# A decoder layer on one core: self attention's order within a period, and where cross attention's first pair begins

## The reference

```
x = x + self_attn(layernorm(x))               # scores / 4 + bias, causal, softmax, values, Wo
q, k, v = layernorm(x) @ Wq + bq, ctx @ Wk + bk, ctx @ Wv + bv
out = softmax(q k^T / 8) v @ Wo + bo + layernorm(x)
x = x + layernorm(out) * gamma + beta
x = x + fp8(layernorm(x)) @ fp8(kernel) + bias
```

## Time and profile before

| | |
|---|---|
| time, median of 3 runs | 1931.88 us (1915.99 to 1938.19) |
| the profiled execution, its time | 1929.99 us |
| its span | 1928.2 us |
| PE busy | 1758.9 us (91%) |
| DVE, ACT, POOL busy | 1289.3, 921.8 and 974.3 us |
| mean granted TensorE clock | 0.947 of full speed |

### The profile page before, as it was taken

How to read it: one execution, slowest core, us unless ns; L and a number is a source line. 1 busy time by engine, 2 the same in 40 slices (tenths; PEclk the granted TensorE clock), 3 DMA queues, 4 the chain that set the end, 5 groups by cost and what they waited for, 6 DMA issues and landing times.

```text
span 1928.2 us, 29741 instructions
## 1 busy us (share of the span) xinstructions
PE 1758.9 (91%) x10650; PEld 886.1 (46%) x10650; DVE 1289.3 (67%) x2503; ACT 921.8 (48%) x1866; POOL 974.3 (51%) x824
## 2 busy tenths in 40 slices
PE   7989988988998999999999999999999999999962
PEld 3544444434444544445545545545544554554421
DVE  5677777766733557756756655665665665678998
ACT  2346667656765243244444444445445445445531
POOL 1000000000001466558888888898898898882244
PEclk9879999889988899899999999999999999999985
DMA  4232311250011000000000000000000000000001
GB/s 115 35 36 36 35 18 19 36 98 2 1 47 42 11 0 1 1 11 4 1 10 4 1 10 4 1 11 1 4 10 1 4 1 1 4 11 23 1 28 38
DMA packets 29129, 34.48 MB, mean 18 GB/s; under 512 B 4290, under 2 KB 27139, under 8 KB 27523
## 3 DMA queue, kind: packets, MB, share of 16 engines
q1 hardware_dynamic: 28984, 32.59, 9.1%
HBM read 14.99 MB, written 4.19 MB: 10 GB/s over the span
## 4 chain that ended last, share of the span: by engine, by line
PE 76%; DVE 16%; issue 3%; ACT 3%; SPq 1%; POOL 1%; DMA 0%; POOLq 0%; ACTq 0%; DVEq 0%
PE psum L964 17%; PE psum L944 14%; PE psum L929 9%; DVE maxima L1229 8%; PE psum L850 7%; PE psum L762 6%; PE psum L800 4%; PE psum L825 4%; PE psum L987 3%; PE psum L917 3%; PE psum L862 2%; PE psum L975 2%; DVE parts_room L1323 1%; DVE stack_room L1279 1%; PE psum L877 1%
## 5 line engine op out<-in xcount | busy, mean ns | idle before, releaser
L1229 DVE TENSOR_REDUCE maxima<-psum 128x1 f32<-128x400 f32 (+5 forms) x1664 | 858.8, 578 | 315.2 <-PE psum L929 214.3
L737 POOL TENSOR_TENSOR parts_room<-parts_room,weights_room 128x512 f32<-128x512 f32 (+1 forms) x565 | 705.6, 1279 | 141.3 <-ACT weights_room L1119 141.3
L1119 ACT ACTIVATE weights_room<-psum 128x512 f32<-128x512 f32 (+1 forms) x757 | 405.8, 599 | 500.2 <-PE psum L944 423.4
L1047 ACT ACTIVATE weights_room<-psum 128x512 f32<-128x512 f32 (+3 forms) x640 | 300.1, 534 | 178.1 <-PE psum L825 99.5
L1436 POOL TENSOR_SCALAR rstd<-meanvar 128x2 f32<-128x2 f32 (+1 forms) x24 | 8.2, 343 | 650.7 <-DVE meanvar L1179 650.7
L944 PE MATMUL psum<-stack_room,dk_hi 64*128 64x512 f32 (+1 forms) x1408 | 264.5, 410 | 4.9 <-ACT weights_room L1119 4.8
L929 PE MATMUL psum<-k_later,stack_room 64*128 64x400 f32 (+1 forms) x896 | 243.6, 412 | 22.5 <-DVE stack_room L1279 14.6
L929 PEld LDWEIGHTS psum<-k_later,stack_room 64*128 64x128 f32 x896 | 129.0, 185 | 221.2 <-issue 121.9
L964 PE MATMUL psum<-weights_room,parts_room 128*64 128x512 f32 (+1 forms) x754 | 204.6, 610 | 0.0
L964 PE MATMUL psum<-weights_room,late_room 128*64 128x512 f32 (+1 forms) x760 | 203.9, 609 | 0.0
L825 PE MATMUL psum<-stack_room,stack_room 51*128 51x512 f32 (+3 forms) x640 | 140.1, 437 | 36.6 <-DVE maxima L1229 34.4
(11 more groups left out here) (133 smaller groups left out, 1907.7 us busy)
## 6 DMA issues: line engine op xcount, KB each, us to landing
stack_room<-parts_room SPq DMA_DIRECT2D x84, 128.0 KB
x_block<-x_dram SPq DMA_DIRECT2D x8, 512.0 KB, 4.7
x_middle<-x_block SPq DMA_DIRECT2D x4, 512.0 KB, 3.2
x_block<-x_middle SPq DMA_DIRECT2D x4, 512.0 KB, 3.8
out_dram<-x_block SPq DMA_DIRECT2D x8, 256.0 KB, 2.1
stack_room<-parts_room SPq DMA_DIRECT2D x24, 64.0 KB
parts_room<-ctx_dram SPq DMA_DIRECT2D x1, 1536.0 KB
stack_room<-shift_rows SPq DMA_DIRECT2D x64, 2.0 KB
```

Source lines behind the costliest of these rows:

```text
L737: engine.tensor_tensor(sum_[:kw, :], old[:kw, :], weights[u % NP_WEIGHTS][:kw, :], ALU.add) \
L1047: engine.activation(w_self[s % NW][:, m, 0:n], bank_of(use + m)[:, 0:n], ACT.Exp, scale=SELF_SCALE).then_inc(emptied(use + m), 1)
L1119: engine.activation(weights[u % NP_WEIGHTS][:kw, :], pair_scores[u % NSCORES][:kw, :], ACT.Exp, scale=CROSS_SCALE).then_inc(pair_exp, 1)
L1229: engine.tensor_reduce(maxima[:, p % 2, i // TB, n, i % TB, ch:ch + 1], bank_of(use + n)[:, 0:real - k0], AX.X, ALU.max) \
```

## The change

In pairs 1 to 6 of self attention both chunks of a period now stand between the two scores and the values, where one stood ahead of each of the scores. Beside self's last pair now lie: cross attention's keys of pair 0 (from the fifth step on), and in the second half the turning of block 0's normalised rows into a buffer of their own (`early_turn`, `first_rows`, since `norm_t` still holds self's output), block 0's queries of pair 0, and the 16 chunks of block 0. The clearing of the keys' last columns is a stage of its own (`key_pads`). The keys' rests, the clearing of the shifts, the row of shifts of block 0 and the turning of blocks 1 and 2 stay between the two attentions. The queries of blocks 1 to 3, the turning of block 3 and the bias of `resid` move beside block 0 of cross, and pair 1's keys and queries from beside block 0 to beside block 1. The waits of the copies follow the buffers that they write.

```diff
@@ -178,7 +178,15 @@
     def self_out(self, b):
         for half in range(2):
             self.put("self_project", b, half, banks=1)
-        self.after(2, lambda: self.put("self_norm", b))
+        self.after(2, lambda: self.self_norm(b))
+
+    def self_norm(self, b):
+        self.put("self_norm", b)
+        self.normed = b
+
+    def early_turn(self, c):
+        assert self.normed >= 0
+        self.put("early_turn", c, banks=1)
 
     def sweep2(self, p):
...
 
-    def pair_keys(self, p):
+    def pair_keys(self, p, rests=True):
         steps = []
         for b in range(NK):
             steps.append((1, lambda b=b: self.put("project_keys", p, b, banks=1)))
+            if not rests:
+                steps.append((0, lambda b=b: self.put("key_steps", p, b)))
+                continue
             for kind, late in (("key_steps", 1), ("key_rests", 2)):
                 if b >= late:
                     steps.append((0, lambda kind=kind, b=b - late: self.put(kind, p, b)))
-        return steps + [(0, lambda kind=kind, b=b: self.put(kind, p, b))
-                        for kind, b in (("key_steps", NK - 1), ("key_rests", NK - 2), ("key_rests", NK - 1))]
+        ends = (("key_steps", NK - 1), ("key_rests", NK - 2), ("key_rests", NK - 1)) if rests else ()
+        return steps + [(0, lambda kind=kind, b=b: self.put(kind, p, b)) for kind, b in ends]
+
...
@@ -370,27 +386,34 @@
                                for b in range(-(-S // BQ)) for c in range(DC)]
 
                 main = self.sweep2(p)
-                self.spread(main, self.mingled(self.sweep1(p + 1), context), [n for n in range(len(main)) if n % 3 < 2])
+                self.spread(main, self.mingled(self.sweep1(p + 1), context), range(2, len(main), 3))
             else:
-                self.interleave(self.sweep2(p), [])
+
+                main = self.sweep2(p)
+                half = next(n for n, m in enumerate(main) if m[2] == HT)
+                put("key_pads")
+                self.spread(main[:half], self.pair_keys(0, rests=False), range(TB, half))
+                queries = self.pair_queries(0)
+                early = [(1, lambda c=c: self.early_turn(c)) for c in range(DC)] + queries[:1] \
+                    + self.pair_sweep1(0, [0], rows=False)
+                self.spread(main[half:], early, range(2 * TB, len(main) - half))
         while self.pending or self.soon:
             self.values()
 
-        def now(steps):
-            for _, step in steps:
-                step()
-
+        put("pair_rows", 0, 0, banks=1)
         put("cross_start")
         self.step = 0
-        now(self.pair_keys(0))
-        for b in range(NB):
-            for c in range(DC):
-                put("resid_turn", b, c, banks=1)
-        put("resid_bias")
-        now(self.pair_queries(0) + self.pair_sweep1(0, [0], waits=True))
-
-        sides = [self.pair_tiles(0) + self.pair_sweep1(0, [1]) + self.pair_keys(1) + self.pair_queries(1),
-                 self.pair_sweep1(0, [2]) + self.pair_sweep1(1, [0]), self.pair_sweep1(0, [3]) + self.pair_sweep1(1, [1]),
+        for b in range(NK):
+            put("key_rests", 0, b)
+        for b in range(NB - 1):
+            for _, step in self.resid_turn(b):
+                step()
+        rows = [(0, lambda: put("pair_rows", 0, 1, banks=1))]
+
+        sides = [self.pair_tiles(0) + queries[1:2] + self.pair_sweep1(0, [1], rows=False) + self.resid_turn(NB - 1)
+                 + [(0, lambda: put("resid_bias"))] + rows + queries[2:],
+                 self.pair_sweep1(0, [2]) + self.pair_keys(1) + self.pair_queries(1) + self.pair_sweep1(1, [0]),
+                 self.pair_sweep1(0, [3]) + self.pair_sweep1(1, [1]),
                  self.mingled(self.pair_sweep1(1, [2, 3]), self.pair_tiles(1))]
         for p in range(NP):
...
@@ -649,13 +676,19 @@
     dk_hi, dk_lo = zip(*[(sb(f"dk_hi{i}", [P, S - APART], F32R), sb(f"dk_lo{i}", [P, S - APART], F32R))
                          for i in range(2)])
 
+
     late_room = Room(nc, sb, "late_room", NS * P * 4)
-    k_first, k_later = late_room.take([SE], F32R), sb("k_later", [P, SE], F32R)[:, :]
+    assert late_room.first >= slopes_at[0] and late_room.first + late_room.size <= slopes_at[1]
+    shifts = sb("shifts", [P, NB, BQ], F32R)
+    later_room = Room(nc, sb, "later_room", -(-SE * 4 // 32) * 32)
+
+    first_rows = later_room.take([DC, BQ], F32)
+    k_first, k_later = late_room.take([SE], F32R), later_room.empty().take([SE], F32R)
+    assert later_room.first >= slopes_at[2]
     v_pair = [v_pair0, late_room.empty().take([NS, P], F32)]
 
     spare = context.rearrange("p t d -> p (t d)")
     k_whole, dk_whole = spare[:, 0:S], spare[:, SE:SE + S - APART]
-    shifts = sb("shifts", [P, NB, BQ], F32R)
     middle = nc.dram_tensor("x_middle", (T, D), F32, kind="Internal").ap()
 
...
@@ -903,9 +936,11 @@
                         pe.wait_ge(*bank_read(use_of["context_turn", NB - 1, c]))
                     project(use, lambda kc: wk2[p % 2][:, kc, :], lambda kc: ctx_t[:, kc, k0:k1], k1 - k0)
                 else:
+                    first = (p, b) == (0, 0)
                     for c in range(DC):
-                        pe.wait_ge(*bank_read(use_of["resid_turn", b, c]))
-                    project(use, lambda kc: wq2[p % 2][:, kc, :], lambda kc: norm_t[:, kc, block(b)], BQ)
+                        pe.wait_ge(*bank_read(use_of[("early_turn", c) if first else ("resid_turn", b, c)]))
+                    project(use, lambda kc: wq2[p % 2][:, kc, :],
+                            lambda kc: first_rows[:, kc, :] if first else norm_t[:, kc, block(b)], BQ)
             elif kind == "value_tiles":
                 p, n = at
...
@@ -1068,6 +1103,9 @@
                 b, c = at
                 rows = min(BQ, S - b * BQ)
                 turned(use, ctx_t[:, c, b * BQ:b * BQ + rows], rows)
+            elif kind == "early_turn":
...
@@ -1078,11 +1116,13 @@
                 act.wait_ge(small_in, 16 * 2)
                 if p >= 2:
                     act.wait_ge(pair_scored, pair_last(p - 2))
+                elif kind == "project_queries":
+
+                    act.wait_ge(*scores_made(last_step(NP - HP + p, NB - 1)))
                 else:
 
-                    act.wait_ge(*scores_made(SELF_STEPS - 1))
-                    act.wait_ge(values_done, SELF_STEPS)
-                    act.wait_ge(*bank_filled(use_of["self_project", NB - 1, 1]))
+                    for c in range(DC):
+                        act.wait_ge(*bank_filled(use_of["context_turn", -(-S // BQ) - 1, c]))
                 if kind == "project_keys":
                     k0, k1 = KEY_BLOCKS[b]
                     if p:
@@ -1101,6 +1141,12 @@
                 p, b = at
                 k0, k1 = apart(b)
                 act.wait_ge(*bank_read(use_of["project_keys", p, b]))
+                if p >= 2:
+                    act.wait_ge(pair_scored, pair_last(p - 2))
+                else:
+
+                    act.wait_ge(values_done, SELF_STEPS)
+                    act.wait_ge(*bank_filled(use_of["self_project", NB - 1, 1]))
                 engine.copy(dk_hi[p % 2][:, k0 - APART:k1 - APART], dk_whole[:, k0 - APART:k1 - APART]) \
                     .then_inc(apart_made, 1)
...
@@ -1436,15 +1482,18 @@
                 chain.on(engine.tensor_scalar(rstd[:, sl], meanvar[:, sl, 1], LN_EPS, None, ALU.add))
                 after_last()
                 engine.tensor_tensor(rstd[:, sl], rstd[:, sl], minus_half[:, sl], ALU.pow).then_inc(rstd_ready, 1)
+            elif kind == "key_pads":
+
+                for c in range(DC):
+                    pool.wait_ge(*bank_filled(use_of["context_turn", -(-S // BQ) - 1, c]))
+                chain.on(engine.memset(k_later[:, S:SE].bitcast(F32), 0.0))
+                after_last()
+                engine.memset(k_first[:, S:SE].bitcast(F32), 0.0).then_inc(pads_cleared, 1)
             elif kind == "cross_start":
 
                 pool.wait_ge(values_done, SELF_STEPS)
                 pool.wait_ge(*bank_filled(use_of["self_project", NB - 1, 1]))
                 engine.drain()
-
-                for k in (k_first, k_later):
-                    chain.on(engine.memset(k[:, S:SE].bitcast(F32), 0.0))
-                    after_last()
                 engine.memset(shifts[:, :, :].bitcast(F32), 0.0).then_inc(shifts_cleared, 1)
                 pool.wait_ge(shifts_cleared, 1)
```

24 lines of the change are left out of this document (17 added, 7 removed).

## The result

The changed kernel takes **1940.87 us** (median of 20 runs, 1930.15 to 1949.42), the kernel before 1923.71 (20 runs, 1912.75 to 1940.93). The ratio is 1.0083, with a 95% interval of 1.0058 to 1.0108: some 16 us slower, where 7 us faster had been forecast. The profiled execution took 1948.07 (span 1946.3, mean granted clock 0.938; before 1928.2 and 0.947).

The account below looks back on a forecast made before the run. PE, busy 91% of the span, was taken as the bound, so its waits count. Terms -5 - 32 + 20 + 6.6 + 1.4 + 2 = -7 us on 1929.99 gave 1923, with an 8-in-10 range of 1904 to 1941.

Parts of the forecast that it names:

- The order in self's pairs 1 to 6: Self's pairs 1 to 6: PE waits for an exponential instead of a maximum, 0.09 us sooner in 9 periods a pair; -5 us.
- The bank count: Full self periods: the second chunk's last bank is that of the first scores, so PE waits for the first exponential; period 2.7.
- +4, if the copy costs each of the 24 finishing periods 0.4: Upper bound of the -5 for self's pairs 1 to 6: ACT's copy costs 0.4 us each time and half the gain goes.
- Between the attentions: From self's last output product to first cross scores: keys, queries and maxima leave, POOL's chain then limits; -32 us (-33 to -29).
- Self's last pair: Added keys, transposes, queries and 16 chunks, plus PE's waits and low clock, lengthen it by 20 us (+8 to +25).
- both stands: Self's last pair: PE waits 4.3 and 4.4 us for maxima queued behind `self_norm` on DVE; with low clock some 12 us.
- The 2.7 us of low clock: Self's last pair: low stretch behind the old 1.28 us wait at 581.88, taken off the sum as going with that wait.
- Blocks 0 and 1: Cross attention's first two blocks: moved queries and transposes, closer maxima and a later row of shifts; +10 us.
- The queries and transposes: Cross blocks 0 and 1: three projections of queries (5.3) and 8 transposes (1.4) come in from between the attentions; +6.6 us.
- the row: Cross block 1: its row of shifts, issued on SP behind `pair_load`'s four transfers, arrives late; +2 us (0 to +3).
- block 1 has 40 side steps in the room of 32: Cross block 1: pair 1's keys and queries only move there, but maxima come closer together; +1.4 us (0 to +5).
- the burst: Rival: four products in a row make PE wait for the second exponential, 0.5 us over 72 full periods; +36, 1959 us; chance 0.10.

Follow-up runs that it names:

- experiment 1: Kernel before with only the new order of self's pairs 1 to 6 (both chunks between scores and values): 1937.41 us, ratio 1.0068 to the kernel before.
- experiment 9: Kernel before with the new order only in the two periods of each self pair behind the copies of blocks 0 and 1: 1944.08 us, ratio 1.0109.
- experiment 10: Kernel before with the new order only in the other eighteen periods of each self pair, not the two behind the copies: 1926.05 us, ratio 0.9993.
- experiment 7: Kernel before with the loads for cross attention behind the first shift rows of pair 6 in SP's list: 1920.09 us, ratio 0.9966.
- experiment 8: Changed kernel with old order behind the copies, norms split in two, block 1's row before pair 2's loads, cross loads behind pair 6's first shift rows: 1917.60 us, 0.9965.
- experiment 11: Changed kernel with old self order, split norms, pair 1's keys and queries in block 0, block 1's row earlier, cross loads later: 1908.75 us, ratio 0.9911 to before.
- experiment 6: Changed kernel with keys and queries of pair 1 back at the end of block 0's side work: 1932.26 us, ratio 1.0047 to the kernel before.
- experiment 5: Changed kernel with the row of block 1's shifts issued ahead of the loads of pair 2's weights on SP: 1940.67 us, ratio 1.0095 to the kernel before.
- experiment 2: Changed kernel with the old order in self's pairs 1 to 6: 1937.63 us, ratio 1.0035 to the kernel before.

## Why the prediction was wrong, by its own steps

- **The order in self's pairs 1 to 6: -5 forecast, +12 to +13 measured (experiment 1). This is the step that failed**, and it carries 17 of the 23 us between forecast (-7) and result (+16). The bank count was right (2.70 us, PE waits for the first exponential), and so was "less three in which ACT first copies a block's product". What failed is its price: "+4, if the copy costs each of the 24 finishing periods 0.4". The copy costs 0.7 to 0.8 in two of a pair's four finishing periods with no clock lost, and low clock follows the wait in pairs 2 to 5, which the term left out though the last pair's term had it. The wait is shown by its rows, the place by experiments 9 and 10. That the low clock follows from the wait is not shown pair by pair, since the same period is followed by full clock in pair 1.
- Inside this term a gain was missed as well: the stand of 7.22 us behind SP's queue in pair 5 (experiment 7). I had read no period of pair 5.
- **Between the attentions: -32 forecast, -33.0 measured** (42.4 to 9.4 us, from the end of the product), with POOL's chain as the limit, as worked out. The 41.6 us of the prediction start 0.8 later, at PE's next instruction. Where before is undisturbed (experiments 1, 7 and 10) it is 41.5 to 41.6 from the product's end, so -32.2.
- **Self's last pair: +20 forecast.** In the profile +15, inside the bounds, with both stands at their forecast length. But the baseline was bad: the last pair of before had 24 us of low clock in its profile. Where no low clock falls, the old last pair takes 61.1 us (experiments 1, 7 and 10), not 71.3, and the new one 77.2 even without the long stands (experiments 8 and 11, with 7 us of low clock). Against such a run the term is +25, its upper bound. The 2.7 us of low clock that the sum took off as going with the old wait were a disturbance of that profile: the same waits (1.72, 1.27 and 1.27 for `o_raw`) stand in the last pair of experiment 1, and its clock never falls.
- **Blocks 0 and 1: +10 forecast, +18 measured.** The queries and transposes (+6.6) and the row (+2, measured 1.82) hold roughly: with keys and queries back the sum is 102.7, which is +6 against the profile of before (96.7, 10 of it at low clock in block 1) and +10 against the undisturbed 92.3 of experiments 1, 7 and 10. What failed besides is "block 1 has 40 side steps in the room of 32", +1.4 (0 to +5): it cost 12 us in the profile and 9 in the median (experiment 6), nearly all of it low clock.
- **The sum**: by the experiments it is +12 for the order and +7 (1 to 13) for all the rest, of which the stands are 10 and the keys 9, against -32 between the attentions. They add to the +16 measured within their intervals. The profiles agree when all kernels that share a stretch are taken together: the last pair is 64.6 us on the mean of five old ones and 86.8 of five new ones, blocks 0 and 1 are 93.2 and 112.7 (five and four), the stretch between is 42.2 and 9.8. That is +22.2 + 19.5 - 32.4 = +9 for the rest.
- **The rivals.** The one that came true in its sign was the burst (+36, at 0.10), though not by its mechanism: PE waits for the first exponential in a full period, and eighteen periods of burst show no cost (experiment 10). Its limit, 0.1 us over the 72 full periods, was not met: they became 0.09 shorter. Against the rival I had only the bank count, which speaks of full periods and was right there.
- **The range.** That 1940.87 is still inside it (1941) is luck. It was set around a kernel before at 1931.88, the median of three runs, and allowed 9 us over that; the kernel before is at 1923.71 and the change is +16. The prediction also took 1% as the least that can be told from no change; with 20 runs of each kernel the interval is 0.25% to each side.
- **Small slips in the sum.** Three projections and 8 transposes add to 6.7, not 6.6. The order's upper bound of +4 does not follow from its terms: 24 x 0.4 less half of the 5 is +7. Neither would have covered +12.

## What to carry to other kernels

When an order is changed for its full periods, work out the odd ones first (those with a copy or a fold): a copy that moves ahead of the result that PE waits for costs up to its length (0.8 of 1.05 us here), and low clock may follow. That is here the larger part: the 0.66 us by which undisturbed pairs differ would be 4 us in six pairs, of +12. Cost each stretch against several executions, one of them undisturbed, since one profile's low clock is no property of the kernel. And a move that "only moves" work is not free if it packs more side work into a block: here that cost 12 us in the profile.

## What the runs showed of the hardware

Nearly all the spread between runs of one kernel goes with the granted clock. Of the 31 runs of the kernel before that were taken beside experiments 5 to 8 the fastest took 1911.22 us at a mean clock of 0.960, the slowest 1944.18 at 0.936; a line through all gives 12.3 us for each 0.01, with a correlation of -0.96. That is a relation between runs, and no experiment set the clock by itself. It also covers the loss of the new order: alone it has a mean clock of 0.9409 (12 runs) against 0.9498 of before (35 runs), and 0.0089 is 11 us by that slope, of 12 measured. It does not cover every difference between kernels. Experiment 7 has 0.9514 against 0.9501 and gains 7 us, where the slope gives 2; experiment 8 has 0.9498 against the same 0.9501 and gains 8.

The Trainium skill, "TensorE: Matmul & The Clock Gate", section "Part 1: The HAM clock gate (the "warmup" mystery)", says that the number of slow products at a kernel's start varies from run to run, and puts the penalty of that ramp under 1% of a typical span. The variation agrees: the stretch up to self's pair 1 has 24 to 72 us of low clock over the 14 profiles. The 1% speaks of the start alone, and would mislead here: the low clock comes again through the kernel, 204 us of it by the mean of 0.947 over 1928.2 us. At most half of that, 5% of the span, is lost, since some of it falls where PE has little to do (busy 9.95 of the last 48 us, at 0.54).

What stays open is which executions get the low clock behind a wait of a given length. In the kernel before, the period of 3.84 or 3.85 us behind the copy is followed by one of 2.87 or so, at full speed, in pairs 1, 2, 3 and 5 of the profile; in experiment 2, with the same order, it is followed by one of 4.1, partly at half speed, in pairs 1, 2 and 3. No run here tells what decides between the two.
